# Reordering the last sequence of a two-layer model kernel: level weights, end additions, halves of the projection, and the order of the stores

## The reference

```python
# layer 0, per sequence
xz = x @ W_in; xi, z = split(xz)              # selective scan with decay A_bar
y  = (C * scan(A_bar, B * xi) + D * xi) * silu(z) @ W_out
x1 = y + top-1 expert FFN of the normalised y  # 8 experts, gelu
# layer 1, "attention": 16 heads, decay times a level weight, no softmax
W[t,s] = (q_t . k_s) / 8 * exp(cg_t - cg_s) * Lam[t, level(t, s)]   # level: dyadic block of s seen from t
Y  = W @ V
o  = Y @ Wout.T + x
att = layernorm(o) * ln_g + ln_b
# layer 1, recurrent cell, carried from sequence to sequence (T = 16 steps here)
c  = sigmoid(f) * c + sigmoid(i) * tanh(g)
out = tanh(x @ wo.T + c_last @ uo.T + bo) + residuals
```

## Time and profile before

| | us |
|---|---|
| median of three runs | 1060.34 (1059.51 to 1061.62) |
| the profiled execution, its own time | 1059.19 |
| its span (first to last instruction or transfer) | 1057.4 |

### The profile page before, as it was taken

One profiled execution on the slowest core, in us unless ns is written; L12 is line 12 of the kernel. 1 busy time (PEld: TensorE's weight loads), 2 busy tenths in 40 slices (PEclk: granted clock), 3 DMA queues, 4 the chain that ended last, 5 costly groups with the idle time before them and its releaser, 6 DMA issues. The chain is left out here.

```text
span 1057.4 us, 20086 instructions
## 1 busy us (share of the span) xinstructions
PE 1010.9 (96%) x6700; PEld 676.2 (64%) x6700; DVE 891.1 (84%) x2122; ACT 705.8 (67%) x1525; POOL 162.0 (15%) x171
## 2 busy tenths in 40 slices
PE   7899999999999999999999999999999999999984
PEld 4666757666675766757576675766667576675753
DVE  6797897979889797997979889797988979799686
ACT  4693957849486593957749395683948659395692
POOL 0020110111101011110201111011110101111076
PEclk9999999999999999999999999999999999999997
DMA  4000000000000000000000000000000000000526
GB/s 153 20 3 11 2 20 11 0 30 0 20 10 20 10 0 30 0 20 10 0 30 0 30 0 20 10 0 30 0 20 10 17 12 0 30 0 20 179 76 193
DMA packets 31908, 27.62 MB, mean 26 GB/s; under 512 B 1552, under 2 KB 25744, under 8 KB 31760
## 3 DMA queue, kind: packets, MB, share of 16 engines
q1 hardware_dynamic: 31888, 27.37, 8.0%
HBM read 15.57 MB, written 11.80 MB: 26 GB/s over the span
## 5 line engine op out<-in xcount | busy, mean ns | idle before, releaser
L1013 ACT ACTIVATE gx<-p 128x512 f32<-128x512 f32 x256 | 145.9, 596 | 11.5 <-PE p L552 6.9
L1829 POOL TENSOR_TENSOR vp<-vdw,e 128x256 f32<-128x256 f32 (+3 forms) x80 | 60.7, 789 | 556.7 <-ACT e L1062 556.7
L550 PE MATMUL p<-x1Th,Gl 128*128 128x512 f32 x256 | 119.9, 468 | 0.3 <-ACT gx L1013 0.3
L961 ACT ACTIVATE gelu<-p,bias_u 128x512 f32<-128x512 f32 x32 | 22.0, 688 | 124.5 <-PE p L493 124.5
L552 PE MATMUL p<-x1Th,Gh 128*128 128x512 f32 x256 | 100.8, 394 | 0.0
L551 PE MATMUL p<-x1Tl,Gh 128*128 128x512 f32 x256 | 100.2, 391 | 0.0
L672 PEld LDWEIGHTS p<-vbd,pair 128*128 128x128 f32 x512 | 62.0, 191 | 40.4 <-issue 26.8
L612 PEld LDWEIGHTS p<-rs,GT 128*128 128x128 f32 x512 | 60.8, 192 | 21.4 <-ACT ms L1094 13.4
L672 PE MATMUL p<-vbd,pair 128*128 128x128 f32 x512 | 73.3, 286 | 0.0
L626 PE MATMUL p<-gx,x1T 128*32 128x512 f32 x512 | 68.2, 604 | 2.0 <-ACT gx L1013 0.8
L967 ACT ACTIVATE sm<-mv 128x4 f32<-128x4 f32 x32 | 6.6, 205 | 92.0 <-DVE mv L1338 91.7
(11 more groups left out here) (277 smaller groups left out, 2609.9 us busy)
## 6 DMA issues: line engine op xcount, KB each, us to landing
xin<-in_x SPq DMA_DIRECT2D x16, 256.0 KB, 2.8
hx_scratch<-vdw SPq DMA_DIRECT2D x15, 256.0 KB, 2.6
res_scratch<-res SPq DMA_DIRECT2D x14, 256.0 KB, 2.1
gx<-in_weights SPq DMA_DIRECT2D x1, 1216.0 KB, 9.4
vp<-hx_scratch SPq DMA_DIRECT2D x4, 256.0 KB, 3.6
GT<-res_scratch SPq DMA_DIRECT2D x4, 256.0 KB, 3.7
out<-vp SPq DMA_DIRECT2D x4, 256.0 KB, 3.4
W<-in_weights SPq DMA_DIRECT2D x1, 746.0 KB, 10.6
```

The lines of the kernel that those rows point to most:

```text
L550: pe.matmul(head_bank(h)[:, :], tile(Gl, h), x1Th[:, :], start=True, stop=False)
L1013: act.activation(tile(gx, h, T), head_bank(h)[:, :], ACT.Copy).then_inc(R["gx_copied"], 1)
L1829: last = pool.tensor_tensor(view(vp[:, at:at + 128 * count], "p (s h e) -> p s h e", s=count, e=HD), spread(v.unsqueeze(1), [128, count, H ...
```

## The change

Six things move; no arithmetic is added or left out.

1. ACT: `level_distance` and `level_decay` come straight after the first two gates, before the third gate and before head 4. `pair_distance` of tile n is put between pairs of head copies.
2. DVE: `recurrence` comes before `lam_sum` and `fold_own`; `level_weights` comes behind `fold_own`; `cell_out` comes before `node_rows`. PE's `cell_out` comes after all 16 heads, not after 13.
3. POOL: `last_residual` comes first. The end's sums and additions are interleaved. POOL has sequences 6 to 14 to add, DVE 0 to 5 and 15.
4. ACT does the tanh in the order `END_TANH`, and its copies of the turned `yt` (one per half) stand in it.
5. The last sequence's turn, projection, addition, statistics and norm are done in two halves of 256 columns, the first before tile 3 is finished.
6. SP stores in another order; the stores of 13 and 14 stand behind the halves of 15.

```diff
-        POOL_ADDS = 9
+        END_DVE = (0, 1, 2, 3, 4, 5, 15)
+        END_POOL = tuple(range(6, 15))
+        END_SUMS = END_DVE + END_POOL
+        END_TANH = (0, 1, 6, 7, 2, 8, 9, 3, 10, 11, 12, 4, 13, 14, 5, 15)
...
+        END_BANKS = (P0[0], P0[1]) * 3 + (P1[0],)
...
# SP
-                for b in range(POOL_ADDS):
-                    sp.wait_ge(R["end_pool_add"], b + 1)
-                    store(b, whole, end_hx[b])
-                for b in range(POOL_ADDS, B - 1):
-                    sp.wait_ge(R["end_add"], b + 1 - POOL_ADDS)
+                for b in (0, 1, 6, 2, 7, 3, 8, 9, 10, 4, 11, 5, 12):
+                    if b in END_POOL:
+                        sp.wait_ge(R["end_pool_add"], END_POOL.index(b) + 1)
+                    else:
+                        sp.wait_ge(R["end_add"], END_DVE.index(b) + 1)
                     store(b, whole, end_hx[b])
                 for half in range(2):
-                    sp.wait_ge(R["end_add"], B - POOL_ADDS + 1 + half)
+                    sp.wait_ge(R["end_add"], len(END_DVE) + 1 + half)
                     store(B - 1, slice(2 * half, 2 * half + 2), end_hx[B - 1])
+                    sp.wait_ge(R["end_pool_add"], END_POOL.index(13 + half) + 1)
+                    store(13 + half, whole, end_hx[13 + half])
...
# PE
+            def last_turn(half, bank):
+                pe.wait_ge(R["w_ready"], 4 * B)
+                pe.wait_ge(R["yt_ready"], 4 * (B - 1) + 2 * half + 2)
+                for n in range(2):
+                    mm = pe.transpose(tile(bank, n), tile(yt, 2 * half + n), ident)
+                mm.then_inc(R["ytT_ps"], 1)
+
+            def last_project(half, bank):
+                pe.wait_ge(R["ytT_ready"], B + half)
+                for n in range(2):
+                    mm = pe.matmul(tile(bank, n), tile(ytT, 2 * half + n), w("WoutT"), start=True, stop=True)
+                mm.then_inc(R["wo_ps"], 1)
...
-                heads(i, 4, 13)
+                heads(i, 4, H)
                 cell_out()
-                heads(i, 13, H)
...
+                for n in range(3):
+                    pair_scores(i, n + 1)
+                    chunk_values(i, n)
+                    levels(i, n)
                     chunk_sums(i, n)
-                turn_out(i)
-                project_out(i)
+                last_turn(0, P1[2])
+                levels(i, 3)
+                chunk_values(i, 3)
+                last_project(0, P0[2])
+                chunk_sums(i, 3)
+                last_turn(1, P1[1])
+                last_project(1, P1[2])
...
# ACT
             def end_tanh(b):
-                act.wait_ge(R["end_sum"], b + 1)
-                if b >= POOL_ADDS + 3:
-                    act.wait_ge(R["end_add"], b - 2 - POOL_ADDS)
+                act.wait_ge(R["end_sum"], END_SUMS.index(b) + 1)
+                turn = END_DVE.index(b) if b in END_DVE else 0
+                if turn == 6:
+                    act.wait_ge(R["lev_ready"], 4 * B)
+                elif turn >= 2:
+                    act.wait_ge(R["end_add"], turn - 1)
...
                 recurrence(i, 1)
-                heads(i, 4, 6)
-                recurrence(i, 2)
-                heads(i, 6, 8)
                 level_distance(i)
                 level_decay(i)
-                heads(i, 8, 11)
-                heads(i, 11, H)
-                pair_distance(i, 0, TILES)
+                recurrence(i, 2)
+                for n in range(TILES):
+                    heads(i, 4 + 2 * n, 6 + 2 * n)
+                    pair_distance(i, n, n + 1)
+                heads(i, 12, H)
...
-                for b in range(B):
+                for b in END_TANH[0:12]:
                     end_tanh(b)
-                project_out(i)
+                last_copy(0, P1[2])
+                for b in END_TANH[12:B]:
+                    end_tanh(b)
                 logs()
-                rstd2(i)
+                last_copy(1, P1[1])
+                last_rstd(0)
+                last_rstd(1)
...
# DVE
                 pair_differences(i)
+                recurrence(i)
+                dve.wait_ge(R["c_ready"], B)
                 lam_sum(i)
                 fold_own(i)
-                recurrence(i)
-                dve.wait_ge(R["c_ready"], B)
+                level_weights(i)
                 node_lams(i)
+                cell_out()
                 node_rows(i)
-                cell_out()
...
-                level_weights(i)
...
+                for n in range(3):
+                    own_heads(i, n)
+                    pair_weights(i, n + 1)
+                    level_sum(i, n)
+                    if n == 2:
+                        end_add(2)
+                    tile_sum(i, n)
+                    end_add((0, 1, 3)[n])
+                level_products(i, 3)
                 own_heads(i, 3)
+                level_total(i, 3)
+                last_attention_out(0)
                 tile_sum(i, 3)
+                last_stats(0)
+                for b in (4, 5, B - 1):
                     end_add(b)
+                last_attention_out(1)
+                last_stats(1)
+                last_norm(0)
+                last_out(0)
+                last_norm(1)
+                last_out(1)
...
# POOL
+                last_residual()
                 finish(i - 1)
                 level_values(i)
-                last_residual()
...
-                for b in range(9):
+                for b in END_SUMS[0:10]:
                     end_sum(b)
                 pool.wait_ge(R["end_loaded1"], 16 * 6)
-                for b in range(9, B):
+                end_sum(9)
+                for b in range(10, 15):
+                    end_add(b - 4)
                     end_sum(b)
-                for b in range(POOL_ADDS):
+                for b in range(11, 15):
                     end_add(b)
```

More of the change, by code:

```diff
@@ L1589, in pair_weights, with level_runs, level_products @@
                     .then_inc(R["w_ready"], 1)
-            def level_sum(i, n):
+            def level_runs(n):
+                return [[(0, 0, 2)], [(0, 0, 3)], [(0, 0, 2), (2, 3, 1)], [(0, 0, 4)]][n]
+            def level_products(i, n):
                 dve.wait_ge(R["lev_ps"], 4 * i + n + 1)
@@ L1595, in level_sum @@
                 al = view(alpha[:, :], "p (l k h) -> p k l h", l=4, k=TILES)[:, n]
-                runs = [[(0, 0, 2)], [(0, 0, 3)], [(0, 0, 2), (2, 3, 1)], [(0, 0, 4)]][n]
-                for at, level, count in runs:
+                for at, level, count in level_runs(n):
                     o = view(lv[:, 128 * at:128 * (at + count)], "p (l h e) -> p l h e", l=count, e=HD)
@@ L1602, in level_sum, with level_total @@
                 last.then_inc(R["lev_ready"], 1)
+            def level_total(i, n):
                 dve.wait_ge(R["lev_ready"], 4 * i + n + 1)
-                count = sum(r[2] for r in runs)
+                count = sum(r[2] for r in level_runs(n))
                 dve.tensor_reduce(lvs[:, :], view(lv[:, 0:128 * count], "p (l v) -> p v l", l=count), AX.X, ALU.add)\
                     .then_inc(R["levsum_ready"], 1)
+            def level_sum(i, n):
+                level_products(i, n)
+                level_total(i, n)
             def own_heads(i, n):
@@ L1737, in stages, with last_attention_out, last_stats, last_norm @@
                     recurrence(i)
-            def last_attention_out():
-                dve.wait_ge(R["wo_ps"], B)
+            def last_attention_out(half):
+                cols = slice(256 * half, 256 * half + 256)
+                dve.wait_ge(R["wo_ps"], B + half)
                 dve.wait_ge(R["res_ready"], B - 1)
-                dve.tensor_tensor(ob[:, :], P1[1][:, :], xn1[:, :], ALU.add).then_inc(R["ob_ready"], 1)
-            def last_norm():
-                dve.wait_ge(R["mv2_ready"], B)
-                for n in range(TILES):
+                dve.tensor_tensor(ob[:, cols], (P0[2], P1[2])[half][:, 0:256], xn1[:, cols], ALU.add).then_inc(R["ob_ready"], 1)
+            def last_stats(half):
+                dve.wait_ge(R["ob_ready"], B + half)
+                for n in (2 * half, 2 * half + 1):
+                    last = dve.bn_stats(st2[:, 6 * n:6 * n + 6], tile(ob, n))
+                last.then_inc(R["st2_ready"], 1)
+                dve.wait_ge(R["st2_ready"], B + half)
+                for n in (2 * half, 2 * half + 1):
+                    last = dve.bn_aggr(mv2[:, 2 * n:2 * n + 2], st2[:, 6 * n:6 * n + 6])
+                last.then_inc(R["mv2_ready"], 1)
+            def last_norm(half):
+                dve.wait_ge(R["mv2_ready"], B + half)
+                for n in (2 * half, 2 * half + 1):
                     last = dve.scalar_tensor_tensor(tile(skip, n), tile(ob, n), mv2[:, 2 * n:2 * n + 1], w("lng"),
@@ L1751, in last_norm, with last_out @@
                 last.then_inc(R["n_ready"], 1)
-                dve.wait_ge(R["r2_ready"], B)
-                dve.wait_ge(R["n_ready"], B)
-                dve.wait_ge(R["end_add"], B - POOL_ADDS)
-                for n in range(TILES):
```

(14 more changed lines are left out.)

49 lines of the change are left out of this document (14 added, 35 removed).

## The result

The changed kernel takes 1053.95 us (median of 4, 1053.15 to 1054.38) against 1059.92 us for the one before (median of 4, 1058.83 to 1061.62): ratio 0.9943, 95% interval 0.9931 to 0.9955, 6.0 us less. Forecast were 4.6 us less, 1055.7.

A forecast was written before the change was run, and what follows sets the result against it. The end was taken as an engine chain to 1051.06 us plus a store backlog; 2.3 us less on the chain and 2.4 on the backlog made -4.7 of span, and the median 1060.34 - 4.6 gave 1055.7, range 1053.3 to 1058.7.

The forecast's parts named there:

- likeliest case: Whole kernel: the forecast's own case, 1055.7 us, own range 1054.5 to 1056.7, chance 0.52.
- case 3: Whole kernel: more is gained, with stall 1.9 and last landing after 2.3; 1054.3 us or a little less, chance 0.08.
- POOL's start: Last sequence's front: DVE's copy of the cell's output over at 1015.0, so POOL starts at 1015.1, 2.1 us earlier.
- sum of six terms: DVE's front: recurrence 2.05, lam_sum and fold_own 2.26, weights 0.9, node_lams 2.95, loss to POOL 2.6, copy 0.6; 11.4 us.
- Strict alternation: Front: DVE and POOL exclude each other for all five operations, 4.2 us in place of 2.6; 1057.3 us, chance 0.2.
- S: Start of POOL's 25 end operations: 1017.23 before, forecast 1015.1.
- The middle: DVE's tiles: last tile_sum at 1040, between 1039 and 1043.6; decides only if later than ACT's last copy.
- ACT's queue: Second half: last copy waits behind POOL's 21st operation, three tanh and a table load, over at 1044.2; this queue decides.
- DVE's end: End of the engines' chain: DVE's last operation at 1048.8 instead of 1051.06, 2.3 us less.
- The stores: SP's queue: stores start at about 1029 instead of 1038; backlog behind DVE's end 6.3 to 3.9, 2.4 us less.
- The coupling: Ring of ACT, DVE and POOL: POOL pauses some 3 us, gain falls to about 1.5; 1058.8 us, chance 0.13.
- The clock: PE's four tiles: clock falls earlier, +7.5 us on the last tile_sum; 1063.2 us, slower, chance 0.07.

The follow-up runs named there:

- e4_late: Changed kernel with ACT's level distance and decay put back behind head 7; 1053.85 us, ratio 0.9940 to the kernel before.
- res_late: Changed kernel with POOL's last_residual put back behind level_values; 1055.18 us, ratio 0.9964 to the kernel before.
- w_late: Changed kernel with level_weights put back behind the pair products; 1053.32 us, ratio 0.9945 to the kernel before.
- copy_early: Changed kernel with ACT's copy of the second half moved ahead of the tanh of 14, 5 and 15; 1053.19 us, ratio 0.9951 to the kernel before.
- b_cell: Kernel before with one edit, DVE's cell_out ahead of node_rows; 1057.18 us against 1059.49, ratio 0.9981.
- whole: Changed kernel with the last turn, projection, statistics and norm in one piece again; 1056.97 us against 1060.33 for the kernel before, ratio 0.9970.
- st_asc: Changed kernel with SP storing 0 to 14 in ascending order, then the halves of 15; 1056.19 us, ratio 0.9976 to the kernel before.
- st_1314: Changed kernel with the stores of 13 and 14 ahead of the halves of 15; 1052.55 us, ratio 0.9941 to the kernel before.
- w_both: Changed kernel with w_late, copy_early and st_1314 together; 1053.37 us, ratio 0.9938 to the kernel before.
- both: Changed kernel with copy_early and st_1314 together; 1051.39 us (median of 6), ratio 0.9938 to the kernel before.
- changed: The changed kernel run again, unedited, in a second set; 1053.85 us, ratio 0.9944 to the kernel before.
- w_st: Changed kernel with w_late and st_1314 together; 1053.65 us, ratio 0.9942 to the kernel before.

## Why the prediction was right

The direction and the whole range (1053.3 to 1058.7) held. The measured 1053.95 lies 0.5 us below the likeliest case's own range of 1054.5 to 1056.7, at the number of case 3 (1054.3 or a little less, chance 0.08). But what case 3 was to come from did not happen: the loss to POOL was 2.4 and not 1.9, and from the last issue to the span's end it took 3.3 us, where the forecast had 3.4. The steps are those of the forecast's own case, and the front was better than forecast. Half a microsecond is the earlier mark. By its steps:

- **POOL's start.** Forecast 2.1 us earlier, measured 2.86 (18.40 to 15.54 from the mark). The sum of six terms was 11.4; from the free end of the pair differences to the end of the copy it measured 10.65. Three were too high: the weights 0.66 (I had 0.9), `node_lams` with its copy 2.59 (2.95, from a line through two other operations), the loss to POOL 2.4 (2.6; it is 0.9 in the last pair difference, 1.2 in the cell, 0.3 in `lam_sum`).
- **Strict alternation**, the second case (S at 1016.7, chance 0.2). Its price did not come, but its pattern did. Taken one by one, POOL's last four operations and DVE's pair difference stand like this:

```profile
1002.50 1.57 DVE L1620 TENSOR_TENSOR pair<-pair,cgt 128x512 f32<-128x512 f32 x1
1003.48 1.08 POOL L1885 TENSOR_TENSOR vp<-vdw,e 128x256 f32<-128x256 f32 x1
1004.52 0.85 POOL L1885 TENSOR_TENSOR vp<-vdw,e 128x128 f32<-128x128 f32 x1
1005.34 1.30 POOL L1885 TENSOR_TENSOR vp<-vdw,e 128x384 f32<-128x384 f32 x1
1006.60 1.08 POOL L1885 TENSOR_TENSOR vp<-vdw,e 128x256 f32<-128x256 f32 x1
```

  With DVE's starts at 1003.99, 1005.03, 1005.96 and 1007.22 (above) the two engines take turns from the first operation to the last, and each record is longer than it is in the loop or without a neighbour. What was too high is the 4.2 that the case asked for this. POOL's 4.24 in the kernel before is already longer than the 3.75 to 3.84 of the loop's passes, and only a part of POOL's time was lost to DVE: 2.4, while POOL itself grew to 5.53. In e4_late DVE lost 2.5, POOL took 3.73. So one `level_values` cost DVE about 2.5 us at both places, and what POOL itself pays depends on the DVE operations that it meets. The forecast's 2.6 was chosen between two bounds, nearer to the loop; that it came within 0.2 while the engines alternated as in the rival is in part luck.
- **The middle.** Forecast tile 3 at 1040, measured 1038.39, 1.1 earlier from the mark and at the best that the forecast thought possible; off the path, as said (`res_late`: summed 2.06 later, with no loss beyond what S explains). Of what the early weights do there I had the sign open; they were a loss of 0.6 on the whole (w_late).
- **ACT's queue.** Forecast: POOL's 21st operation, three tanh, table load, copy, over at 1044.2. Measured 1042.95, earlier by 1.25, and S was earlier by 1.23 than forecast (0.5 of it the earlier mark). PE 1.22 for 1.04, DVE 3.66 for 3.45. copy_early takes that queue away and gains.
- **DVE's end.** Forecast -2.3, measured -2.64 from the mark. One reading under it was wrong: "The chain of engines goes back to POOL" does not hold for the kernel before, where `b_cell` shows DVE's end hanging on the tiles. It did no harm, since the forecast took 1051.06 from the trace and worked out only the new chain. In the changed kernel DVE's end does follow S (`res_late`, `w_late`). So the gain is not S's 2.86 passed on: the tiles came 3.73 earlier and made room, and S sets how much of that is used. whole puts 1.83 of it on the halves; the parts are not to be added up.
- **The stores.** Forecast -2.4 behind DVE's last operation, measured -2.5 (6.3 to 3.8); st_asc puts 2.1 on the order. The two stores held behind the halves cost 1.1 (st_1314), named in the forecast and left unpriced there. Three small slips in the forecast's text move nothing: no engine works from 1051.06 on, not from 1050; the earlier trace rows has 3.7 as the longest landing, not 3.0; and the terms add up to 4.7, of which the last step takes 4.6.
- **The coupling.** POOL ran its 25 operations without a pause, 1013.87 to 1044.30; the fourth case did not happen.
- **The clock.** 1.00 up to 1040 in the changed kernel; the fifth case did not happen. b_cell and res_late each show a fall of 3.4 us in the middle of the work, worth 1.5 and 2.1 us on the tiles; neither reached the end of the span by more than about 0.1.

The forecast was 4.7 us of span and the trace says 5.2 less from the mark, 5.7 with the mark's own shift of 0.5. That shift is not part of the change: the profiles of kernels with the same loop have the mark from 997.8 to 999.4 (and two later, below). The 6.0 of the medians stands on such scatter too.

## What to carry to other kernels

Where an engine's queue ends in a table load or a wait for a slow engine, ask what urgent small step stands behind it: moving one 0.38 us copy ahead was worth 1.2 us. Order stores by when their data are ready and put the largest ones that are ready ahead of the last result, until the transfers have no gap left; in w_both, where none was left, engines that were done 0.5 us earlier than in both gained nothing. An operation that runs slowly beside another engine is only worth moving if its new place is not on the path: 4.1 us in slack were cheaper than 0.66 us ahead of the start of the chain (`w_late`). But slack belongs to one arrangement: with the early copy and the earlier stores of 13 and 14, the same late weights made the kernel a microsecond slower (`w_both` against `both`).

## What the runs showed of the hardware

- **DVE and POOL.** The same two operations on 128 columns took 0.58 and 1.60 us (changed, copy_early), the same four on 64 columns 0.66 and 4.1 to 4.5, according to whether POOL was busy. In the changed kernel's front the two engines' starts alternate one by one. The Trainium skill ("SBUF — State Buffer", section "Who interferes with whom") has it as an exclusive hold for the length of the instruction; these rows agree. That POOL's side pays too is seen in `level_values`: 3.73, 4.24 and 5.53 us beside short, mixed and long DVE operations.
- **The clock.** In b_cell the granted clock was 0.50 from 1030.4 to 1033.6, in the middle of the tiles, after PE had been busy 0.23 of 2 us. In res_late it was 0.50 from 1018.1 to 1021.4, after PE had been busy 0.71 of 2 us. The kernel before was busy 0.73 of the 2 us from 1028 to 1030 and kept 1.00.
- **Two starts.** In two profiles of fourteen (w_late and w_st) the whole program runs 3 us late from the first sequence on. The line of the token transpose, in the changed kernel and in w_late (least, median and longest ns, first and last start):

```profile
L1606 DVE STREAM_TRANSPOSE pair<-cgt x16: 2311/2311/2312, 57.3 to 998.3; 128x2048 f32<-128x2048 f32 x16
```
```profile
L1606 DVE STREAM_TRANSPOSE pair<-cgt x16: 2311/2312/2312, 60.5 to 1001.5; 128x2048 f32<-128x2048 f32 x16
```

The first is at 57.3 and 60.5, the last at 998.3 and 1001.5: the difference is all there before the loop's second pass. In the other profiles the first is at 56.6 to 58.5. Executions 3 us above their kernel's median stand in several sets (both: 1054.2 and 1054.6 beside 1051.0 to 1051.5). What delays the start stays open. For a change of a few microseconds, a mark inside the trace told more than the times of five executions.
